# Transposed rows by DMA instead of TensorE in the expert stage of a cross-attention and expert-choice kernel

## The reference, cut to what matters

```python
x = x + xattn(layernorm(x), ctx)            # x: (2, 2048, 512), 8 heads, 77 context rows
n = layernorm(x)
scores = n @ gate_w.T                       # 8 experts
probs = softmax(scores)
g, m = top_k(probs.transpose(0, 2, 1), 512) # each expert takes 512 rows of each batch
xin = n[batch, m]                           # (2, 8, 512, 512)
h = gelu(xin @ w1)                          # w1: (8, 512, 2048)
h = h @ w2                                  # w2: (8, 2048, 512)
out = x + scatter_add(g[..., None] * h, m)
```

## Time and profile before

| | us |
|---|---|
| median of three runs | 1684.53 |
| the profiled execution | 1684.68 |
| its span, first to last instruction | 1683.0 |
| PE busy | 1668.5 |
| DVE busy | 1089.1 |
| ACT busy | 828.5 |
| POOL busy | 347.4 |

### The profile page before, as it was taken

The page is one execution under the profiler, slowest core; times in us unless marked ns, Lnnn a source line. Parts: engine busy times, 40 slices in busy tenths (PEclk is TensorE's granted clock), DMA queues, the critical chain, the costliest instruction groups (busy, mean ns, idle before and its releaser), DMA issues.

```text
span 1683.0 us, 23464 instructions
## 1 busy us (share of the span) xinstructions
PE 1668.5 (99%) x8732; PEld 1427.8 (85%) x8732; DVE 1089.1 (65%) x2010; ACT 828.5 (49%) x1931; POOL 347.4 (21%) x412
## 2 busy tenths in 40 slices
PE   9999999999999999999999999999999999999997
PEld 8999999878888888888888888888888888888886
DVE  7555797877766657555755575557555755675663
ACT  5677777633333334444644454445444544454441
POOL 4223334111121113300340034003300430041002
PEclk9999999999999999999999999999999999999999
DMA  3243445334344243411341134113411431142003
GB/s 132 76 151 104 147 138 211 133 109 126 125 107 169 59 142 124 127 51 50 76 125 51 50 78 123 51 51 83 118 50 51 87 114 51 51 88 63 25 1 50
DMA packets 76678, 156.40 MB, mean 93 GB/s; under 512 B 4461, under 2 KB 5641, under 8 KB 76569
## 3 DMA queue, kind: packets, MB, share of 16 engines
q1 hardware_dynamic: 62201, 121.36, 21.2%
q0 software_dynamic: 14336, 33.56, 10.0%
q10 hardware_dynamic: 32, 0.03, 0.0%
HBM read 121.38 MB, written 33.55 MB: 92 GB/s over the span
## 4 chain that ended last, share of the span: by engine, by line
PE 97%; ACT 1%; DVE 1%; DMA 0%; POOL 0%; issue 0%; POOLq 0%; SPq 0%
PE ps L2089 10%; PE ps L2088 10%; PE ps L2087 10%; PE ps L2067 9%; PE ps L2066 9%; PE ps L2065 9%; PE ps L1228 4%; PE ps L1229 4%; PE ps L1230 4%; PE ps L1978 4%; PE ps L1965 3%; PE ps L1980 3%; PE ps L1967 3%; PE ps L1979 3%; PE ps L1966 3%; PE ps L2024 1%
## 5 line engine op out<-in xcount | busy, mean ns | idle before, releaser
L2087 PE MATMUL ps<-v2h,hhS 128*128 128x512 f32 x768 | 300.5, 391 | 0.0
L2089 PE MATMUL ps<-v2h,hlS 128*128 128x512 f32 x768 | 298.9, 389 | 0.0
L2088 PE MATMUL ps<-v2l,hhS 128*128 128x512 f32 x768 | 298.9, 389 | 0.0
L2065 PE MATMUL ps<-Th,Wh 128*128 128x512 f32 x672 | 261.4, 389 | 0.0
L2066 PE MATMUL ps<-Tl,Wh 128*128 128x512 f32 x672 | 261.4, 389 | 0.0
L2067 PE MATMUL ps<-Th,Wl 128*128 128x512 f32 x672 | 261.4, 389 | 0.0
L1523 POOL DMA_INDIRECT out_dram<-YS,tok_idx x48 | 82.9, 1728 | 804.9 <-DVE YS L1887 796.5
L1669 ACT ACTIVATE v2h<-w_raw 128x512 fp32r<-128x512 f32 x96 | 57.5, 623 | 308.7 <-PE ps L2089 308.7
L1887 DVE SCALAR_TENSOR_TENSOR YS<-ps,tok_gate,YS 128x512 f32<-128x512 f32 x144 | 106.8, 750 | 132.1 <-PE ps L2089 132.1
L2089 PEld LDWEIGHTS ps<-v2h,hlS 128*128 128x128 f32 x768 | 144.2, 188 | 29.7
L2088 PEld LDWEIGHTS ps<-v2l,hhS 128*128 128x128 f32 x768 | 144.3, 188 | 29.3
(11 more groups left out here) (281 smaller groups left out, 3592.2 us busy)
## 6 DMA issues: line engine op xcount, KB each, us to landing
w_raw<-in_L_ffn_w_dram SPq DMA_DIRECT2D x80, 1024.0 KB, 5.6
XB<-in_x_dram SPq DMA_DIRECT2D x16, 512.0 KB, 4.1
XR<-in_x_dram SPq DMA_DIRECT2D x16, 512.0 KB, 6.2
out_dram<-X SPq DMA_DIRECT2D x16, 512.0 KB, 5.1
xn_rows<-XN SPq DMA_DIRECT2D x16, 512.0 KB, 5.4
w_raw<-in_L_xattn_Wq_dram SPq DMA_DIRECT2D x1, 1024.0 KB, 8.8
wo_sb<-in_L_xattn_Wo_dram SPq DMA_DIRECT2D x2, 512.0 KB, 11.2
w_raw<-in_L_xattn_Wk_dram SPq DMA_DIRECT2D x1, 768.0 KB, 5.3
```

The lines of the kernel that those rows point to most:

```text
L2065: nc.tensor.matmul(ps[:, bank, :], wh, th, start=(idx in OPENS and k == 0), stop=False, **go_on)
L2087: nc.tensor.matmul(ps[:, bank, :], th, wh, start=(t == 0), stop=False)
L2088: nc.tensor.matmul(ps[:, bank, :], th, wl, start=False, stop=False)
L2089: last = nc.tensor.matmul(ps[:, bank, :], tl, wh, start=False, stop=(t == GF - 1))
```

## The change

Fourteen of the sixteen columns no longer pass TensorE to be turned (`TURNED`: plain columns 1 and 3, and the 12 columns of the pairs). Plain columns 0 and 2 stay. A turned column takes these steps:

1. ACT reads the gathered rows as 16-bit halves and writes them as separate planes (`act_split`, two instructions of 128x1024 for each half a of the rows).
2. SP issues one transposing DMA of 128x2048 16-bit elements, 512 KB, for each a (`sp_turn`).
3. ACT waits for it and writes the halves back into `rows_in` as 32-bit words, turned (`act_words`, four instructions of 128x512 for each a).
4. ACT and DVE make high and low parts and the sums from `rows_in` in SBUF, as instructions of 128x1024 for pairs (`t_block`, `t_sum`, `t_high`, `t_low`). GpSimd does none of it.

For pairs the planes lie in raw weight buffers: those of column b of pair x + 1 in the `w2_raw` and `w1_raw` of group g = 1 + b of expert x. So SP loads the weights of the group two later only behind that turn. The splits and words stand at the end of ACT's groups g = 1 and g = 2. In the last group the blocks are prepared from the third product on.

```diff
+        TURNED = ((1,), (3,), (0, 1), (0, 0)) + tuple((x, b) for x in range(1, NS) for b in range(B))
...
+        def act_split(key, a):
+            rows = rows_of(key).bitcast(U16).rearrange("p q (d h) -> p h q d", h=2)
+            halves = planes_of(key)[0]
+            for h in range(2):
+                last = nc.scalar.activation(halves[:, 2 * a:2 * a + 2, h * D:(h + 1) * D],
+                                            rows[:, h, 2 * a:2 * a + 2], ACT.Copy)
+            last.then_inc(r_split, 1)
+
+        def sp_turn(sp, key, a):
+            halves, out = planes_of(key)
+            sp.wait_ge(r_split, turned(key) - 1 + a)
+            sp.dma_start(out[:, a * 4 * CAP:(a + 1) * 4 * CAP].rearrange("p (j t) -> p j t", t=P),
+                         halves[:, 2 * a:2 * a + 2].rearrange("p q c -> p (q c)"), transpose=True).then_inc(r_turn[a], 16)
+
+        def act_words(act, key, a):
...
+            act.wait_ge(r_split, turned(key))
+            act.wait_ge(r_turn[a], 8 * turned(key))
+            for h in range(2):
+                for q in range(2):
+                    last = nc.scalar.activation(words[:, h, 2 * a + q], out[:, h, q], ACT.Copy)
+            last.then_inc(r_word, 1)
...
+        SPLIT_AT, WORDS_AT, CHUNKS_AT = (10, 11), (12, 13), {13: (0,), 14: (1,), 15: (2, 3)}
+        PAIR_SPLIT_AT = {(0, 1): (49, 50), (0, 0): (52, 53)}
+        PAIR_WORDS_AT = {(0, 1): (51, 52), (0, 0): (54, 55)}
...
             for n in range(NG):                                    # sp_experts
                 e, g = NPE + n // G, n % G
+                key = ((n - 2) // G + 1, (n - 2) % G - 1) if n >= 2 else None
+                if key in TURNED:
+                    sp.wait_ge(s_Wl, NPR * (n - 2) + 3)
+                    sp.wait_ge(s_sum, 4 * (n - 1))
+                    for a in range(2):
+                        sp_turn(sp, key, a)
+                    sp.wait_ge(r_word, turned(key))
...
                 sp.dma_start(w1_raw[:, n % 2], group_w1(e, g)).then_inc(s_raw1[n % 2], 16)
...
-                        if x + 1 < NS and j in (3, 5):             # pool_experts
-                            t_low(x + 1, j // 2 - 1)
...
+                key = (x + 1, g - 1)                               # act_experts, end of group(n)
                 if n + 1 < NG:
-                    for idx in W_ORDER[0:6]:
+                    for idx in W_ORDER[0:3]:
                         w_high(n + 1, idx)
-                    if last:
-                        t_stage(x + 1, 0, T_BANKS[0])
-                    w_high(n + 1, W_ORDER[6])
+                    if key in TURNED:
+                        act.wait_ge(s_rows[key[1]], 16 * CT * (x + 2))
+                        act.wait_ge(s_v2l, GF * (n + 1))
+                        act_split(key, 0)
+                    for idx in W_ORDER[3:]:
+                        w_high(n + 1, idx)
+                    if key in TURNED:
+                        act_split(key, 1)
+                        act_words(act, key, 0)
+                        act_words(act, key, 1)
...
-                    if g == G - 1 and x + 1 < NS and 2 <= j < 6:   # pe_experts
-                        t_stage(x + 1, j - 2, T_BANKS[j % 2])
```

More of the change, by code:

```diff
@@ L10 @@
 U32 = mybir.dt.uint32
+U16 = mybir.dt.uint16
 ACT = mybir.ActivationFunctionType
@@ L1421, in xattn_expert_choice @@
         NU = len(PRODUCTS)
+        LAST_USE = {idx: PRODUCTS.index((idx, 1)) + 1 for idx in range(NPR)}
         HIDDEN = ((0, 0), (0, 2), (1, 1), (1, 3), (0, 1), (1, 0), (0, 3), (1, 2))
@@ new lines, in xattn_expert_choice, with planes_of @@
+        planes = [put(f"planes{i}", (26624, 118784)[i], [P, CT, 2 * D], U16) for i in range(2)]
+        turned_planes = [put(f"turned_planes{i}", (34816, 126976)[i], [P, CT * 2 * D], U16) for i in range(2)]
+        def planes_of(key):
+            if len(key) == 2 and key[0]:
+                m = ((key[0] - 1) * G + 1 + key[1]) % 2
+                return (w2_raw[:, m].bitcast(U16),
+                        w1_raw[:, m].rearrange("p k f -> p (k f)").bitcast(U16))
+            m = key[0] % 2 if len(key) == 1 else 0
+            return planes[m][:], turned_planes[m][:]
@@ L1432, in xattn_expert_choice @@
+        SPLIT_AT, WORDS_AT, CHUNKS_AT = (10, 11), (12, 13), {13: (0,), 14: (1,), 15: (2, 3)}
+        PAIR_SPLIT_AT = {(0, 1): (49, 50), (0, 0): (52, 53)}
+        PAIR_WORDS_AT = {(0, 1): (51, 52), (0, 0): (54, 55)}
         s_raw1 = [sem(f"s_raw1_{i}") for i in range(2)]
         s_raw2 = [sem(f"s_raw2_{i}") for i in range(2)]
-        (s_prod, s_u1, s_c11, s_u2, s_u7, s_c22, s_c21, s_gelu, s_hid, s_sum, s_Wh, s_Wl, s_v2h, s_v2l, s_dn, s_ev, s_tr, s_Ta,
-         s_T2, s_Td, s_Th, s_Tl, s_rows, s_scat) = (sem(f"s_{n}") for n in (
-             "prod u1 c11 u2 u7 c22 c21 gelu hid sum Wh Wl v2h v2l dn ev tr Ta T2 Td Th Tl rows scat").split())
+        (s_prod, s_u1, s_c11, s_u2, s_u7, s_c22, s_c21, s_gelu, s_hid, s_sum, s_Wh, s_Wl, s_v2h, s_v2l, s_dn, s_ev, s_Ta, s_Tb, s_T1,
+         s_T2, s_Td, s_Th, s_Tl, s_scat) = (sem(f"s_{n}") for n in (
+             "prod u1 c11 u2 u7 c22 c21 gelu hid sum Wh Wl v2h v2l dn ev Ta Tb T1 T2 Td Th Tl scat").split())
@@ L1438, in w_block @@
+        s_rows = [sem(f"s_rows{b}") for b in range(B)]
         def w_block(n, idx):
@@ L1649, in w_high, with t_high @@
+            def t_high(x, sums):
+                for idx in sums:
+                    if idx == TT3:
+                        act.wait_ge(s_T1, x + 1)
+                    elif idx == TT2:
+                        act.wait_ge(s_T2, x + 1)
+                    elif idx == TT4:
+                        act.wait_ge(s_Td, x + 1)
+                    nc.scalar.activation(Th[:, idx], Tf[:, idx], ACT.Copy).then_inc(s_Th, 1)
             def w_high(n, idx):
@@ L1710, in group @@
                 keep_u1(n, 1)
+                last = g == G - 1 and x + 1 < NS
+                if last:
+                    t_block(x + 1, B11)
                 hidden(n, 1)
                 keep_u2(n, 0)
+                if last:
+                    t_block(x + 1, B21)
                 w2_high(n, (3,))
@@ L1906, in group @@
                 low(n, 5)
+                if last:
+                    t_sum(x + 1, TT3)
                 if more:
```

243 lines of the change are left out of this document (142 added, 101 removed).

## The result

The changed kernel takes 1665.47 us (median of 4 runs, 1663.86 to 1667.86), against 1684.15 for the kernel before beside it (1683.74 to 1685.67). The ratio is 0.9889, with a 95% interval from 0.9871 to 0.9906: faster by 18.7 us. The forecast was 1660.5, so 5.0 us of its gain are missing: the time lies within the outer range (1657 to 1690) and 0.5 us above the forecast's own (1659 to 1665).

The account below looks back on a forecast made before the run. TensorE, busy 1668.5 of 1683.0 us, was taken to bound the kernel by its instruction count times pace. 1684.68 - 25.0 (TensorE) + 0 + 0.8 (last groups) = 1660.5 us; own range 1659 to 1665, outer range 1657 to 1690.

Parts of the forecast that it names:

- The floor: On PE, removing 24 pair stages (21.4 us) and eight plain-column chunks (3.6) saves 25.0 us, down to 1659.7.
- Plain columns and the first pair: Splits two slots ahead of the words, 10.9 us per transpose, cover it; cost 0, with 0 to 3 us kept.
- ACT in groups g = 1 and g = 2: Splits and words added on ACT sum to 8.5 us against 16.69 idle, so PE does not wait.
- The price of a transpose: Each transposing DMA of 512 KB on SP's queue taken at 6 us, so nothing of it is seen.
- The rival price of 92 ns for each run of 256 bytes: Each short run costs as much as a 2 KB packet: 11.8 us per transpose, two 8.3 us late.
- Rival A: Late transposes delay the words ending groups g = 1 and 2, ten times, and PE stops: about 1743 us; chance 0.20.
- its window: At the pairs, two transposes of a column have 17.3 us before PE waits; each us beyond costs ten.
- The last groups: In groups g = 3, VectorE's added low parts spill over some 2.3 us; cost 0.15 each, 0.8 us in all.
- Rival C: VectorE's low parts make each last group pay 1 to 2.4 us, five times: 1668 us; chance 0.11.
- GpSimd costed at 0: GpSimd loses 69.4 us of work which nobody waited for, so its term is 0.

Follow-up runs that it names:

- the third experiment: Changed kernel with only the low parts of the row sums moved back from VectorE to GpSimd (128x1024 blocks): 1675.73 us.
- the turn first: Changed kernel with SP issuing the first pair's two transposes ahead of that slot group's weight loads: 1661.22 us.
- the last experiment: Changed kernel with the first pair's transposes ahead of the weight loads and plain columns 1 and 3 turned by TensorE again: 1662.75 us.

## Why the prediction was right, and where it was not

**The floor: right.** 25.0 us was forecast for PE. Each last group gives 3.57, to the second decimal, and with the first pair's wait out of the way 24.3 us are gained behind the start, with the 0.8 of `cnt` as the difference. The span's 25.3 has 1.2 us of a shorter start in it.

**The failed step: "Plain columns and the first pair".** It cost the one place with trouble at 0, with 0 to 3 us kept. It named the place (column (0, 0), behind two loads of 1 MB) and then let it go with "PE asks for a slot's Gelu only two slots on". That it has one slot where the others have two is a misreading: in `PAIR_SPLIT_AT` and `PAIR_WORDS_AT` both columns of the first pair have two, and both stand behind loads. Three things were wrong. The transpose was priced as if it ran alone, 6 us, where behind the loads it took 10.7 us to land. The two slots were taken for 10.9 us, but ACT was behind, because it had stood 6.87 us for column (0, 1), and caught up: from the end of the first split (611.58) to the point where it stood before the words (616.52) it had only 4.9 us, and SP spent 2.8 of them in the wait of the loads. And the two slots of slack behind the Gelu were not set against the wait in front of it: ACT stood 8.70 us, the slack covered 5.2, and PE stood for the rest. The price was 3.6 of standstill plus 2.8 to 2.9 at the lower clock, 6.5 us, over twice the bound of 3. Both edits that remove this wait, by order on SP or by place on ACT, bring the median to 1661.22 and 1660.65, within 0.8 us of the 1660.5 forecast. A part of that closeness is luck: the 0.8 us put down for VectorE did not come, and the 0.8 of `cnt`, put down nowhere, did.

**ACT in groups g = 1 and g = 2: right that nothing is seen, one size off.** The splits were put at 1.03 us and take 1.05; the words were put at 0.55 us each (2.19 / 4) and take 0.66 by the same count (2.66 / 4). ACT's timeline of a group g = 2 answers to the earlier trace rows:

```profile
942.83 2.00 ACT L1465 ACTIVATE w_raw<-XR 128x1024 uint16<-128x1024 uint16 x2
944.73 2.19 ACT L1761 ACTIVATE Wh<-Wf 128x512 fp32r<-128x512 f32 x4
946.81 2.00 ACT L1465 ACTIVATE w_raw<-XR 128x1024 uint16<-128x1024 uint16 x2
949.26 2.66 ACT L1482 ACTIVATE XR<-w_raw 128x512 uint16<-128x512 uint16 x4 [0.45 <-DMA w_raw<-w_raw]
953.24 2.66 ACT L1482 ACTIVATE XR<-w_raw 128x512 uint16<-128x512 uint16 x4 [1.32 <-DMA w_raw<-w_raw]
961.71 1.15 ACT L1771 ACTIVATE v2h<-w_raw 128x512 fp32r<-128x512 f32 x2 [5.81 <-PE ps L2218]
```

4.0 + 5.3 = 9.3 us of work, where 8.5 was forecast, under an idle time of 16.69; 5.81 of it is left, and it is still PE that ends it.

**The price of a transpose: the right side, and below the value taken.** 6 us was taken out of 4.1 to 6.2 and 11.8. The median is 4.3. The rival price of 92 ns for each run of 256 bytes is refuted: the queue has 58240 packets more, and its share rose from 21.2% of 1683.0 to 25.9% of 1665.7, over 16 engines 1194 us, or about 21 ns for each short packet, if all of it is put down to them. The prediction's sum for this rival had a slip too: 4.1 less 2.8 is 1.3 us to start and signal, not 2, so two would have taken 24.9 us, and A's price would have been 76 us and not 83. And 13.8 us in the 10.9 of two slots is past the edge, not near it. The Trainium skill's page Advanced Engine Details and Errata (section X-Bar Transpose (TRN2)) has such transposes as fast as ordinary DMAs; the trace agrees, with 4.3 us for 512 KB beside 4.1 and 6.2 for plain ones. Its page VectorE: DVE Perf Modes (section The three transpose paths) has 1309 ns for one 128x128 block; this case shows sixteen in 4.3 us, so the figure is not to be multiplied by the blocks of one DMA.

**Rival A: right in mechanism, absent in size.** Its wait and its place came out when the transposes were tripled (1753.91), and its window was 17.8 us where it had 17.3. Its price for each us was too low, since 6.4 us of idle time cost 8.8. What it had not seen is that the mechanism sits at the first pair too, where the window is far shorter, and how much the clock adds, which it had only named as possible.

**The last groups: right.** VectorE is busy 21.16 of 21.76 us in the second half. What spills over is seen in its timeline behind the start of the next group at 1002.25:

```profile
1003.12 2.35 DVE L1956 TENSOR_TENSOR Tl<-Tf,Th 128x1024 fp32r<-128x1024 f32 x2
1005.39 0.68 DVE L1994 TENSOR_TENSOR hfS<-ps,u 128x512 f32<-128x512 f32 x1
```

The first addition comes 3.14 us behind the start instead of 2.92, and the idle time of the earlier trace rows is used up, as said. The 0.8 us for it was not seen; every group is 40.8. Rival C falls.

**GpSimd costed at 0: right for the wrong question.** Nobody had waited for the 69.4 us that left it. But once the groups are shorter, it would have held VectorE, which the third experiment shows. The prediction had no term for that, since it did not ask what the parts are worth without each other.

By its own last test, "wrong if PE's total idle is over 6 us", the forecast of 1660.5 was wrong: the waits are 3.5 + 1.6 + 1.0 + 1.0 + 0.6 + 0.3 = 8.0 us. The bound was a loose one, for the kernel before has 3.8 us of such waits itself, but the longest of them points to the right place.

**What stays open.** The transposes of column (0, 1) are slow also with the turn first (10.71 us of issue in that kernel, landings of 11.0 and 7.8 us), where no load stands ahead of them in their slot. So the loads are not the only thing that can make a transpose late. It is not peculiar to transposes either: in the kernel before, the load of w1 issued at 590.52 took 13.9 us to land. In the last experiment, where the same two transposes are issued 5.0 us later (593.39 against 588.36), they land in 6.7 and 4.5 us. In the kernel with the turn first GpSimd issues gathers and scatters of a plain column from 575 to 589 us; that they are the cause was not tried. PE never stood right behind these transposes; what they cost is that ACT came late to the words of column (0, 0).

## What to carry to other kernels

Price a transfer at the place in its queue, not by its median elsewhere: behind two 1-MB loads the same transpose took 10.7 us instead of 4.3, and it was issued 2.8 us late because the loads waited for a buffer. The remedy is an order (the small urgent one first) or a wait placed behind the work that the bottleneck needs. When a wait is added on an in-order engine, count the deadline of what is queued behind it at each place where it occurs, the one-off places at the seams too; a standstill of TensorE can cost nearly as much again in clock (here 3.6 us and 2.8). And undo the parts of a change one at a time from both ends: a part that is worth nothing in the old kernel was worth 10 us in the new one.

## What the runs showed of the hardware

- Transposing DMA, SBUF to SBUF, 512 KB of 16-bit words: 4.3 us from issue to landing, of which 1.9 us is the instruction on the issuing queue. Behind two 1-MB loads the two issues took 7.43 and 3.67 us, and the landings 10.7 and 5.1. The page DMA: Bandwidth & Descriptors of the Trainium skill (section Two DMAs through the same engine are not ordered) says that within one queue of one DMA engine descriptors start in order; the late transposes agree with it.
- Copies with 16-bit output at every second word on ACT: 0.77 us for 128x512 (0.66 each in a row of four, 2.66 / 4), where the 32-bit copy of this shape takes 0.62 (0.55, 2.19 / 4). Reading every second 16-bit word cost nothing extra: 1.05 us for 128x1024.
- VectorE beside GpSimd: two subtractions with both inputs in SBUF took 6.71 us instead of 1.33 while GpSimd made two subtractions of 5.33 us together, and one with an input in PSUM kept 0.69. The GPSIMD Engine Reference of the Trainium skill (section 1. Specifications) has the SBUF interface shared for VectorE instructions with two SBUF inputs; the trace agrees.
- TensorE's clock: behind a gap of 3.85 us 13 matmuls ran at a granted 0.50 (1.2 GHz); behind one of 1.97 us the pace stayed that of 2.4 GHz.
